# Selective scan: one product and one recurrence of 1024 columns per group in place of two interleaved halves of each

## The chip, the cores and the metric

One core of a Trainium2 chip runs the whole program. The metric is the device time in microseconds (us) of one execution, and a lower one is better.

## The reference

The program is two layers of a transformer-like net on four sequences of 1024 tokens, 128 features wide: attention and a mixture of experts, then a selective scan (a Mamba-like block) and a second mixture of experts. The change lies in the selective scan, of which this is the core:

```
def _selective_scan(u, A, B_sel, C_sel, delta):
    deltaA = jnp.exp(delta[..., None, None] * A[None, None])
    deltaB_u = delta[..., None, None] * B_sel[:, :, None, :] * u[..., None]

    def step(h, inp):
        a_t, bu_t, c_t = inp
        h = a_t * h + bu_t
        y_t = jnp.einsum('bdn,bn->bd', h, c_t)
        return (h, y_t)
```

For each of 128 features there are 16 states, and each state runs through the 1024 tokens of its sequence by h = a·h + bu. All arithmetic is fp32.

## The kernel before

The scan puts (feature, state) pairs on the 128 partitions and the 1024 tokens of a sequence along the free dimension. A **group** is 8 features × 16 states, so there are 16 groups for each sequence and 64 in all. For group n:

- SyncE loads `x_rep` (the input u, repeated over the states) from memory, one of 5 buffers.
- ScalarE (ACT) makes `da` = exp(delta·A), 1024 columns, three groups ahead, one of 5 buffers (line 2910).
- VectorE (DVE) makes the **product** `ps_bu` = `x_rep` · `ps_b` into PSUM (line 2658); `ps_b` lies in PSUM, `x_rep` in SBUF. It is made in two halves of 512 columns, c = 0 and c = 1.
- VectorE makes the **recurrence** `st` with `tensor_tensor_scan` from `da` (SBUF) and `ps_bu` (PSUM), also in two halves: `first_half` (line 2666) starts from 0, `second_half` (line 2672) from the last column of the first.
- GpSimd (POOL) makes `hc` = `st` · `crep`, 1024 columns, as soon as the whole recurrence of the group is there (line 2929). Both its inputs lie in SBUF.
- TensorE (PE) sums `hc` over the states into `ps_y`, for four groups at a time.

Each engine walks the same list, `scan_plan()`, and takes from it the steps that are its own. Between two groups VectorE has other work, of two kinds. The row statistics (`row_stats`, lines 156 and 160, one SBUF input each) stand in the list after a group's last instruction. The **small steps** are generators on a list `small`: `late_delta` (line 2763, 1024 columns, two SBUF inputs), `deviations` (five operations on 8 columns, lines 2771 to 2783), and the choice of an expert and of a token's place (`choose`, lines 1113 to 1137; `place`, lines 1157 to 1170). `between(3)` runs up to three of them at one point in each group. Most read two SBUF tensors.

The halves are interleaved. For group n VectorE issues: product c = 0 of n, the small steps, second half of n - 1, first half of n, product c = 1 of n. So no instruction needs the one right before it. POOL also issues indirect DMAs (lines 2936 and 1255), the product `brep` · `delta` (line 2947) and `y` · `z` (line 2954) between its `hc` products. At the turn to another sequence ScalarE copies `brep` into `ps_b` (line 2891), and VectorE's next product waits for that.

Of the kernel before, what the change touches and what calls it, by code (L numbers as in the profile page):

```python
# [11 lines left out]
ALU = mybir.AluOpType  # L12
# [4 lines left out]
BATCH, SEQ, HID = 4, 1024, 128  # L17
# [3 lines left out]
BANK = 512  # L21
# [1260 lines left out]
HALF = F0 // 2  # L1282
# [1018 lines left out]
NG = HID // FG  # L2301
NC2 = SEQ // BANK
# [4 lines left out]
NDA, AHEAD, NST_BUF = 5, 3, 4  # L2307

NX, NW = 5, 2
# [105 lines left out]
def selective_scan(nc, sems, a, u_mem, w_tap, w_in, x, h_t, h, spare, wo, marks, weights, loaded, mod_t, gate_bc, ident, eps,  # L2415
# [4 lines left out]
    with ExitStack() as ctx:  # L2420
# [6 lines left out]
        def mark(n, step=1):  # L2427
            return Mark(nc, sems, f"m_{n}", step, marks.pop())

        def sem(n):  # L2430
# [9 lines left out]
        raw, soft, delta = sb("raw"), sb("soft"), [begun_scan[3], sb("delta1")]  # L2440
        x_rep = [sb(f"x_rep{i}") for i in range(NX)]
        brep, crep = sb("brep"), [sb(f"crep{i}") for i in range(2)]
        da, st = [sb(f"da{i}") for i in range(NDA)], [sb(f"st{i}") for i in range(NST_BUF)]
        hc = [sb(f"hc{i}") for i in range(NHC)]
        y = wo[:, :, :, :].rearrange("p k j n -> p (k j n)")
# [11 lines left out]

        w_pe, y_pe = mark("w_pe"), mark("y_pe")

        act, delta_dve, bu_dve, half_dve, scan_dve, y_act = (  # L2460
            mark(n) for n in ("act", "delta", "bu", "half", "scan", "y"))

        y_pool, y_last, delta_b_pool = mark("y_pool"), mark("y_last"), mark("delta_b")

# [9 lines left out]
        for step in plan:  # L2474
            kind, key = step[0], step[1:]
            if step in turn and kind != "conv" or kind == "conv" and key[2] == 0:
                w_pe.add(step)
            if kind in ("u", "z", "raw", "turn") or kind == "rep" and (key[0] or key[1]):
                act.add(step)
            elif kind in ("turn3", "score", "back3", "join"):  # L2480
                act.add(step)
            elif kind == "norm3":
                norm3_act.add(key)
            elif kind == "norm":
                x_norm.add(key)
            elif kind == "soft":
                act.add(step), act.add(step), act.add(step)
            elif kind == "delta":
                delta_dve.add(step)
            elif kind == "delta_b":  # L2490
                (delta_dve if len(key) == 2 else delta_b_pool).add(step)
            elif kind == "b_in":
                act.add(step)
            elif kind == "group":
                for m in (da_act, half_dve, scan_dve, hc_pool):
                    m.add(key)
                for c in range(NC2):
                    bu_dve.add(key + (c,))
            elif kind == "sum":
                y_pe.add(key)  # L2500
            elif kind == "y":
                last_pe.add(key[0])
                for c in range(NC2):
                    for m in (y_act, y_pool) if key[0] < BATCH - 1 else (y_last,):
                        m.add(key + (c,))
            elif kind == "out":
                add_act.add(key)
# [29 lines left out]
        def behind(b, g, by):  # L2537

            n = b * NG + g - by
            return divmod(n, NG) if n >= 0 else None  # L2540
# [106 lines left out]
        def g_first(key):  # L2647
            return key[1] == 0

        def product(e, key, c):  # L2650
            n, cc = key[0] * NG + key[1], HALF[c]
            if c == 0:
                e.wait_ge(x_in[n % NX], (n // NX + 1) * 16)
            if n:

                m = (half_dve, scan_dve)[c]
                e.wait_ge(m.sem, m.at[behind(*key, 1)])
            e.tensor_tensor(ps_bu[:, cc], x_rep[n % NX][:, cc], ps_b[:, cc], ALU.mult).then_inc(bu_dve.sem, 1)  # L2658

        def first_half(e, key):  # L2660
            n, cc = key[0] * NG + key[1], HALF[0]
            e.wait_ge(bu_dve.sem, bu_dve.at[key + (0,)])
            e.wait_ge(da_act.sem, da_act.at[key])
            if behind(*key, NST_BUF):
                e.wait_ge(hc_pool.sem, hc_pool.at[behind(*key, NST_BUF)])
            e.tensor_tensor_scan(st[n % NST_BUF][:, cc], da[n % NDA][:, cc], ps_bu[:, cc], 0.0, ALU.mult, ALU.add).then_inc(half_dve.sem, 1)

        def second_half(e, key):
            n, cc = key[0] * NG + key[1], HALF[1]
            e.wait_ge(bu_dve.sem, bu_dve.at[key + (1,)])  # L2670
            e.wait_ge(half_dve.sem, half_dve.at[key])
            e.tensor_tensor_scan(st[n % NST_BUF][:, cc], da[n % NDA][:, cc], ps_bu[:, cc], st[n % NST_BUF][:, BANK - 1:BANK],  # L2672
                                 ALU.mult, ALU.add).then_inc(scan_dve.sem, 1)

        def vector(e):
            e.wait_ge(loaded, LATER * 16)
# [13 lines left out]
            for step in plan:  # L2690
# [14 lines left out]
                elif kind == "sums":  # L2705
                    b, n = key
# [12 lines left out]
                if kind == "delta" and len(key) == 1:  # L2719
                    small.append(late_delta(e, *key))  # L2720
                elif kind == "delta_b" and key[0] == 0:
                    at, cc = ("rep", 0) + key, part(key)
                    e.wait_ge(w_pe.sem, w_pe.at[at])
                    e.tensor_tensor(ps_b[:, cc], ps_w[turn[at] % NW][:, :], delta[0][:, cc], ALU.mult).then_inc(delta_dve.sem, 1)
                elif kind == "group":

                    if g_first(key):
                        if key[0]:
                            second_half(e, behind(*key, 1))
                        e.wait_ge(*b_ready(key[0]))  # L2730
                        product(e, key, 0)
                    else:
                        product(e, key, 0)
                        between(3)
                        second_half(e, behind(*key, 1))
                    first_half(e, key)
                    product(e, key, 1)
                    if key == (BATCH - 1, NG - 1):
                        second_half(e, key)
                elif kind == "y" and key[0] == BATCH - 1:  # L2740
                    b, = key
                    for c in range(NC2):
                        cc = slice(c * BANK, (c + 1) * BANK)
                        if c < NC2 - 1:
                            e.wait_ge(last_pe.sem, last_pe.at[b])
                        else:
                            e.wait_ge(y_pe.sem, y_pe.at[b, NG // SET - 1])
                        e.wait_ge(w_pe.sem, w_pe.at["out", b - 1, c])
                        e.wait_ge(act.sem, act.at["z", b, c])
                        e.tensor_tensor(y[:, cc], ps_y[c][:, :], z[b % 2][:, cc], ALU.mult).then_inc(y_last.sem, 1)  # L2750
                elif kind == "stats":
                    b, n = key
                    tile = b * TPB + n * 4
                    e.wait_ge(add_act.sem, add_act.at[key])
                    row_stats(e, x, stats, mv, range(tile, tile + 4), row_chain)
                    stats_at[key] = row_chain.n
# [583 lines left out]
```

## Time and profile before

| | us |
|---|---|
| median of 3 runs | 1818.52 (1814.84 to 1818.67) |
| the profiled execution, its own time | 1820.8 |
| its span, first to last instruction | 1819.1 |
| the scan, first product to the start of the last `hc` | 1330.1 to 1600.2 |
| VectorE busy over the span | 1152.2 |
| GpSimd busy over the span | 1346.1 |

The profiled execution is one run of its own, so its stretches are read as durations, and a sum of them is set against its own time. Instructions of VectorE that don't need each other overlap by a few hundredths of a us in the timeline: the next starts before the one before has ended. The distance from start to start is therefore what an instruction takes of the engine, called its pitch below.

### The profile page before, as it was taken

The page shows a single profiled execution, that of the slowest core. Times are in us where ns is not written, and L with a number is a line of the kernel's source. Part 1 is how long each engine was busy: PE and PEld are TensorE (multiplying, and loading weights), DVE is VectorE, ACT ScalarE, POOL GpSimd, SP SyncE. Part 2 cuts the span into 40 slices and gives each one's busy share as a digit, 9 for nine tenths or more (in the row PEclk, how much of TensorE's full clock was granted, in tenths as well). Part 3 has the DMA queues.
Part 4 walks back from the last instruction along what each step waited for, and adds up shares of the span by engine and source line. Part 5 has one row for each costly group of instructions (what it writes and reads, how often), then busy time and mean ns, then how long its engine had stood idle before and what let it go on. Part 6 is the DMA issues. An engine that isn't in the chain of part 4 may idle for free. (4 is left out here: it accounts for less than half of the span.)

```text
span 1819.1 us, 26796 instructions
## 1 busy us (share of the span) xinstructions
PE 1502.0 (83%) x8699; PEld 1034.9 (57%) x8699; DVE 1152.2 (63%) x2579; ACT 797.8 (44%) x1379; POOL 1346.1 (74%) x1154
## 2 busy tenths in 40 slices
PE   5899999999999999999999998988965664357970
PEld 3455556766556755656755657877833232136960
DVE  6866766566676575676566504755589998952224
ACT  2245444345444344444344453444486775323320
POOL 5587988788898698898788783536576657658376
PEclk7699999999999999999999998999977876667995
DMA  6333334231222122131131103024485555424333
GB/s 177 70 89 82 71 71 83 70 70 42 65 58 48 48 56 50 36 70 36 47 70 36 36 13 86 23 72 114 109 199 126 141 133 132 108 69 146 99 86 87
DMA packets 125761, 146.65 MB, mean 81 GB/s; under 512 B 15784, under 2 KB 84796, under 8 KB 125624
## 3 DMA queue, kind: packets, MB, share of 16 engines
q1 hardware_dynamic: 118456, 130.60, 29.3%
q0 software_dynamic: 7168, 14.34, 2.9%
q8 instruction: 72, 1.18, 0.3%
q14 instruction: 65, 0.53, 0.1%
HBM read 65.24 MB, written 29.42 MB: 52 GB/s over the span
## 5 line engine op out<-in xcount | busy, mean ns | idle before, releaser
L838 DVE CUSTOM_DVE_ANT_0 ring<-ring,mask 128x128 f32<-128x128 f32 (+7 forms) x512 | 383.8, 769 | 186.3 <-PE ring L700 185.9
L924 ACT ACTIVATE prob<-ring 128x512 f32<-128x512 f32 x576 | 315.2, 597 | 298.1 <-PE ring L715 294.5
L978 POOL TENSOR_TENSOR acc<-acc,prob 128x512 f32<-128x512 f32 x272 | 353.1, 1298 | 73.0 <-ACT prob L924 49.4
L731 PE MATMUL ps_o<-prob,v 128*64 128x256 f32 x2304 | 282.5, 387 | 3.9 <-issue 3.8
L700 PE MATMUL ring<-k,x 128*128 128x512 f32 (+3 forms) x768 | 252.0, 408 | 35.8 <-ACT prob L924 22.1
L714 PE MATMUL ring<-x,k 128*128 128x512 f32 x576 | 258.1, 448 | 24.6 <-DVE neg_m L838 15.4
L715 PE MATMUL ring<-x,k 128*128 128x512 f32 x576 | 229.4, 398 | 0.0
L700 PEld LDWEIGHTS ring<-k,x 128*128 128x128 f32 x768 | 137.3, 198 | 144.5 <-ACT prob L924 50.9
L731 PEld LDWEIGHTS ps_o<-prob,v 128*64 128x64 f32 x2304 | 154.6, 137 | 106.5 <-issue 39.6
L2929 POOL TENSOR_TENSOR m_hc<-m_st,m_crep 128x1024 f32<-128x1024 f32 x64 | 150.8, 2357 | 71.7 <-DVE m_st L2672 64.0
L975 POOL TENSOR_TENSOR acc<-prob 128x512 f32<-128x512 f32 x144 | 184.4, 1281 | 8.5 <-ACT prob L924 7.2
L945 POOL TENSOR_TENSOR other<-other,sin 128x512 f32<-128x512 f32 x96 | 136.3, 1420 | 59.2 <-DVE other L817 58.6
L714 PEld LDWEIGHTS ring<-x,k 128*128 128x128 f32 x576 | 109.2, 190 | 99.4 <-issue 44.3
L947 POOL TENSOR_TENSOR rot<-rot,other 128x512 f32<-128x512 f32 x96 | 129.2, 1346 | 7.5
L715 PEld LDWEIGHTS ring<-x,k 128*128 128x128 f32 x576 | 109.8, 191 | 19.7 <-issue 7.3
L830 DVE TENSOR_TENSOR rot<-rot,other 128x512 fp32r<-128x512 f32 x64 | 73.2, 1143 | 69.5 <-ACT other L906 69.5
L963 POOL TENSOR_SCALAR_AFFINE_SELECT prob<-prob 128x512 f32<-128x512 f32 x128 | 91.3, 713 | 25.6 <-ACT prob L924 24.5
L816 DVE TENSOR_TENSOR rot<-ring,cos 128x512 f32<-128x512 f32 x96 | 66.3, 690 | 60.1 <-PE ring L682 59.7
L3155 POOL DMA_INDIRECT c_got<-slots_out,f_slot x64 | 65.9, 1030 | 46.3 <-issue 40.6
L743 PE MATMUL ps_l<-acc,v_one 128*64 128x256 f32 x576 | 87.5, 381 | 2.8 <-POOL acc L978 2.7
L1255 POOL DMA_INDIRECT slots_in<-attn_t,f_slot x64 | 63.0, 985 | 31.8 <-issue 15.5
L2658 DVE TENSOR_TENSOR m_ps_bu<-m_x_rep,m_ps_b 128x512 f32<-128x512 f32 x128 | 82.5, 680 | 4.7 <-ACT m_ps_b L2891 4.4
(414 smaller groups left out, 2816.1 us busy)
## 6 DMA issues: line engine op xcount, KB each, us to landing
x<-other SPq DMA_DIRECT2D x256, 128.0 KB, 2.3
m_x_rep<-u_mem SPq DMA_DIRECT2D x64, 512.0 KB, 4.7
x<-rot SPq DMA_DIRECT2D x128, 128.0 KB, 2.3
sorted_in<-zeros SPq DMA_DIRECT2D x3, 1548.0 KB, 11.9
e_sorted<-sorted_in SPq DMA_DIRECT2D x18, 258.0 KB, 3.7
sorted_out<-e_hid SPq DMA_DIRECT2D x18, 256.0 KB, 2.2
slots_in<-zeros SPq DMA_DIRECT2D x2, 2048.0 KB, 8.7
slots_out<-wo SPq DMA_DIRECT2D x16, 256.0 KB, 2.4
```

The lines of the kernel that those rows point to most:

```text
L700: mm = e.matmul(ps[:, c0:c1], x1[g % 2][:, h, qs], k1[g % 3][:, c0:c1], start=True, stop=True)
L714: e.matmul(banks(step, BANK), k1[g % 3][:, ks], x1[g % 2][:, :, qs], start=True, stop=False)
L715: e.matmul(banks(step, BANK), k2[g % 3][:, ks], x2[g % 2][:, :, qs], start=False, stop=True).then_inc(s2_pe.sem, 1)
L731: mm = e.matmul(ps_o[s * D:(s + 1) * D, qb % 2 * 2 * P:(qb % 2 + 1) * 2 * P], v[g % 2][:, kb, :], prob[i % NPROB][:, s * 2 * P:(s + 1) * 2 ...
L838: e.tensor_tensor_reduce(ps, ps, mask_1[:, SEQ - n:SEQ], 1.0, -3.0 * NEG, ALU.add, ALU.min, neg_m[g % 2][:, c, h, qb % QPC:qb % QPC + 1]). ...
L924: e.activation(prob[i % NPROB][:, :], banks(("s2",) + key, BANK), ACT.Exp, scale=-1.0).then_inc(s2_exp.sem, 1)
L945: e.tensor_tensor(other[i][:, :], other[i][:, :], sin[:, cc], ALU.mult).then_inc(rotated.sem, 1)
L947: e.tensor_tensor(rot[i][:, :], rot[i][:, :], other[i][:, :], ALU.add).then_inc(rotated.sem, 1)
L963: e.affine_select(tile[:, :], tile[:, :], [[0, G], [1, P]], ALU.is_ge, 0.0, base=0, channel_multiplier=-1).then_inc(causal.sem, 1)
L975: e.tensor_tensor(total[:, :], first[:, :], tile[:, :], ALU.add).then_inc(summed.sem, 1)
L978: e.tensor_tensor(total[:, :], total[:, :], tile[:, :], ALU.add).then_inc(summed.sem, 1)
L2929: e.tensor_tensor(hc[(b * NG + g) % NHC][:, :], st[r][:, :], crep[b % 2][:, :], ALU.mult).then_inc(hc_pool.sem, 1)
```

## The change

`product` makes all 1024 columns in one instruction, and `states` runs the whole recurrence in one `tensor_tensor_scan` from 0. The product of group n waits for the recurrence of n - 1, which reads `ps_bu`, and the recurrence of n waits for its product. The small steps stay between product and recurrence. The semaphore of the first half is gone. ScalarE, TensorE, GpSimd and SyncE have the same instructions in the same order.

```diff
-        def product(e, key, c):
-            n, cc = key[0] * NG + key[1], HALF[c]
-            if c == 0:
-                e.wait_ge(x_in[n % NX], (n // NX + 1) * 16)
+        def product(e, key):
+            n = key[0] * NG + key[1]
+            e.wait_ge(x_in[n % NX], (n // NX + 1) * 16)
             if n:
-
-                m = (half_dve, scan_dve)[c]
-                e.wait_ge(m.sem, m.at[behind(*key, 1)])
-            e.tensor_tensor(ps_bu[:, cc], x_rep[n % NX][:, cc], ps_b[:, cc], ALU.mult).then_inc(bu_dve.sem, 1)
+                e.wait_ge(scan_dve.sem, scan_dve.at[behind(*key, 1)])
+            e.tensor_tensor(ps_bu[:, :], x_rep[n % NX][:, :], ps_b[:, :], ALU.mult).then_inc(bu_dve.sem, NC2)
 
-        def first_half(e, key):
-            n, cc = key[0] * NG + key[1], HALF[0]
-            e.wait_ge(bu_dve.sem, bu_dve.at[key + (0,)])
+        def states(e, key):
+            n = key[0] * NG + key[1]
+            e.wait_ge(bu_dve.sem, bu_dve.at[key + (NC2 - 1,)])
             e.wait_ge(da_act.sem, da_act.at[key])
             if behind(*key, NST_BUF):
                 e.wait_ge(hc_pool.sem, hc_pool.at[behind(*key, NST_BUF)])
-            e.tensor_tensor_scan(st[n % NST_BUF][:, cc], da[n % NDA][:, cc], ps_bu[:, cc], 0.0, ALU.mult, ALU.add).then_inc(half_dve.sem, 1)
-
-        def second_half(e, key):
...
+            e.tensor_tensor_scan(st[n % NST_BUF][:, :], da[n % NDA][:, :], ps_bu[:, :], 0.0, ALU.mult, ALU.add).then_inc(scan_dve.sem, 1)
...
                     if g_first(key):
-                        if key[0]:
-                            second_half(e, behind(*key, 1))
                         e.wait_ge(*b_ready(key[0]))
-                        product(e, key, 0)
-                    else:
-                        product(e, key, 0)
+                    product(e, key)
+                    if not g_first(key):
                         between(3)
-                        second_half(e, behind(*key, 1))
-                    first_half(e, key)
-                    product(e, key, 1)
-                    if key == (BATCH - 1, NG - 1):
-                        second_half(e, key)
+                    states(e, key)
```

In the listings below a line number is that of the kernel it belongs to; `tensor_tensor_scan` is listed as SCALAR_TENSOR_TENSOR. VectorE in the first sequence, groups with no small steps, before (2658 is a product, 2672 a second half, 2666 a first half):

```order
L2658 TENSOR_TENSOR m_ps_bu<-m_x_rep,m_ps_b 128x512 x2
L2672 SCALAR_TENSOR_TENSOR m_st<-m_da,m_st,m_ps_bu 128x512
L2666 SCALAR_TENSOR_TENSOR m_st<-m_da,m_ps_bu 128x512
L2658 TENSOR_TENSOR m_ps_bu<-m_x_rep,m_ps_b 128x512 x2
L2672 SCALAR_TENSOR_TENSOR m_st<-m_da,m_st,m_ps_bu 128x512
L2666 SCALAR_TENSOR_TENSOR m_st<-m_da,m_ps_bu 128x512
```

The same engine and place in the changed kernel (2654 is the product, 2662 the recurrence):

```order
L2654 TENSOR_TENSOR m_ps_bu<-m_x_rep,m_ps_b 128x1024
L2662 SCALAR_TENSOR_TENSOR m_st<-m_da,m_ps_bu 128x1024
L2654 TENSOR_TENSOR m_ps_bu<-m_x_rep,m_ps_b 128x1024
L2662 SCALAR_TENSOR_TENSOR m_st<-m_da,m_ps_bu 128x1024
L2654 TENSOR_TENSOR m_ps_bu<-m_x_rep,m_ps_b 128x1024
```

Six instructions for two groups became four, each of which needs the result of the one in front of it.

VectorE at the first `deviations` (its five small steps, 2771 to 2783), before. The two products in front of a small step are c = 1 of group n - 1 and c = 0 of group n, and the second half of n - 1 (2672) comes behind the steps:

```order
L2666 SCALAR_TENSOR_TENSOR m_st<-m_da,m_ps_bu 128x512
L2658 TENSOR_TENSOR m_ps_bu<-m_x_rep,m_ps_b 128x512 x2
L2771 SCALAR_TENSOR_TENSOR m_nmr<-mv,m_rstd 128x8
L2774 TENSOR_TENSOR m_nmr<-m_nmr,m_rstd 128x8
L2777 TENSOR_SCALAR m_nmr<-m_nmr 128x8
L2672 SCALAR_TENSOR_TENSOR m_st<-m_da,m_st,m_ps_bu 128x512
L2666 SCALAR_TENSOR_TENSOR m_st<-m_da,m_ps_bu 128x512
L2658 TENSOR_TENSOR m_ps_bu<-m_x_rep,m_ps_b 128x512 x2
L2780 TENSOR_TENSOR m_rstd<-m_rstd,m_nmr 128x8
L2783 SCALAR_TENSOR_TENSOR m_nmr<-mv,m_rstd 128x8
```

The same place in the changed kernel, where the five steps are lines 2753 to 2765:

```order
L2654 TENSOR_TENSOR m_ps_bu<-m_x_rep,m_ps_b 128x1024
L2753 SCALAR_TENSOR_TENSOR m_nmr<-mv,m_rstd 128x8
L2756 TENSOR_TENSOR m_nmr<-m_nmr,m_rstd 128x8
L2759 TENSOR_SCALAR m_nmr<-m_nmr 128x8
L2662 SCALAR_TENSOR_TENSOR m_st<-m_da,m_ps_bu 128x1024
L2654 TENSOR_TENSOR m_ps_bu<-m_x_rep,m_ps_b 128x1024
L2762 TENSOR_TENSOR m_rstd<-m_rstd,m_nmr 128x8
L2765 SCALAR_TENSOR_TENSOR m_nmr<-mv,m_rstd 128x8
L2662 SCALAR_TENSOR_TENSOR m_st<-m_da,m_ps_bu 128x1024
```

The second half of the group before has moved from behind the small steps to a place ahead of the product, so the whole recurrence of n - 1 is complete when that product starts, and the small steps come one instruction of 1024 columns after it.

## Rows read from the trace of the kernel before

**Rows 1.** the page: busy time, share of the span and instructions of each engine

```profile
PE 1502.0 (83%) x8699; PEld 1034.9 (57%) x8699; DVE 1152.2 (63%) x2579; ACT 797.8 (44%) x1379; POOL 1346.1 (74%) x1154
```

**Rows 2.** busy time of each engine in stretches of the scan

```profile
1330.00:1360.00 30.00, 20.58 (x95) 11.35 (x94) 29.80 (x53) 22.77 (x30) 26.04 (x17) 0.88 0.88 207
...
1530.00:1603.00 73.00, 29.63 (x163) 16.10 (x165) 70.66 (x109) 27.80 (x40) 57.59 (x33) 0.66 0.39 103
```

**Rows 3.** waits of VectorE (DVE), 1330 to 1600: us in total, times, longest

```profile
DVE m_ps_bu L2658 <- ACT m_ps_b L2891: 4.4, 2, 2.7
DVE m_delta L2763 <- ACT m_soft L2886: 3.7, 2, 3.2
DVE f_prod L1157 <- PE m_ps_w L1146: 2.3, 1, 2.3
DVE stats L156 <- ACT first_h L2872: 1.7, 1, 1.7
```

**Rows 4.** timeline, VectorE: start us, us, engine, line, operation

```profile
1336.05 1.26 DVE L2658 TENSOR_TENSOR m_ps_bu<-m_x_rep,m_ps_b 128x512 f32<-128x512 f32 x2
1337.22 1.27 DVE L2672 TENSOR_TENSOR_SCAN m_st<-m_da,m_st,m_ps_bu 128x512 f32<-128x512 f32 x1
1338.41 1.19 DVE L2666 TENSOR_TENSOR_SCAN m_st<-m_da,m_ps_bu 128x512 f32<-128x512 f32 x1
1339.53 1.26 DVE L2658 TENSOR_TENSOR m_ps_bu<-m_x_rep,m_ps_b 128x512 f32<-128x512 f32 x2
```

**Rows 5.** single lines, duration in ns as min/median/max

```profile
L2658 DVE TENSOR_TENSOR m_ps_bu<-m_x_rep,m_ps_b x128: 667/678/697, 1330.1 to 1596.3; 128x512 f32<-128x512 f32 x128
L2666 DVE TENSOR_TENSOR_SCAN m_st<-m_da,m_ps_bu x64: 1186/1196/1220, 1330.8 to 1595.2; 128x512 f32<-128x512 f32 x64
L2929 POOL TENSOR_TENSOR m_hc<-m_st,m_crep x64: 2334/2356/2385, 1336.2 to 1600.2; 128x1024 f32<-128x1024 f32 x64
L1130 DVE TENSOR_TENSOR_SCAN f_upto<-f_keep,f_mask x2: 292/292/292, 1480.8 to 1554.6; 128x64 f32<-128x64 f32 x2
L2763 DVE SCALAR_TENSOR_TENSOR m_delta<-m_raw,m_soft x2: 1226/1226/1227, 1368.1 to 1508.7; 128x1024 f32<-128x1024 f32 x2
```

**Rows 6.** timeline, VectorE, a product and what follows without needing it

```profile
1349.96 0.68 DVE L2658 TENSOR_TENSOR m_ps_bu<-m_x_rep,m_ps_b 128x512 f32<-128x512 f32 x1
1350.54 0.86 DVE L156 BATCH_NORM_STATS2 stats<-first_h 128x6 f32<-128x128 f32 x4
```

**Rows 7.** timeline, VectorE, a scan right behind its own product

```profile
1398.87 0.70 DVE L2658 TENSOR_TENSOR m_ps_bu<-m_x_rep,m_ps_b 128x512 f32<-128x512 f32 x1 [2.72 <-ACT m_ps_b L2891]
1399.60 1.22 DVE L2666 TENSOR_TENSOR_SCAN m_st<-m_da,m_ps_bu 128x512 f32<-128x512 f32 x1
```

**Rows 8.** timeline, all engines, small steps beside POOL's product

```profile
1369.20 1.27 DVE L2672 TENSOR_TENSOR_SCAN m_st<-m_da,m_st,m_ps_bu 128x512 f32<-128x512 f32 x1
...
1370.56 2.36 POOL L2929 TENSOR_TENSOR m_hc<-m_st,m_crep 128x1024 f32<-128x1024 f32 x1 [1.49 <-DVE m_st L2672]
...
1371.50 1.27 DVE L2658 TENSOR_TENSOR m_ps_bu<-m_x_rep,m_ps_b 128x512 f32<-128x512 f32 x2
...
1372.68 0.26 DVE L2771 SCALAR_TENSOR_TENSOR m_nmr<-mv,m_rstd 128x8 f32<-128x8 f32 x1
...
1372.97 0.17 DVE L2774 TENSOR_TENSOR m_nmr<-m_nmr,m_rstd 128x8 f32<-128x8 f32 x1
```

**Rows 9.** timeline, all engines, a small step late behind POOL

```profile
1411.51 2.35 POOL L2929 TENSOR_TENSOR m_hc<-m_st,m_crep 128x1024 f32<-128x1024 f32 x1
...
1412.35 1.53 DVE L2771 SCALAR_TENSOR_TENSOR m_nmr<-mv,m_rstd 128x8 f32<-128x8 f32 x1
```

**Rows 10.** timeline, VectorE, the last such pair of small steps

```profile
1579.73 0.27 DVE L2780 TENSOR_TENSOR m_rstd<-m_rstd,m_nmr 128x8 f32<-128x8 f32 x1
```

**Rows 11.** timeline, all engines, the last recurrence and product

```profile
1597.05 1.28 DVE L2672 TENSOR_TENSOR_SCAN m_st<-m_da,m_st,m_ps_bu 128x512 f32<-128x512 f32 x1
...
1600.17 2.36 POOL L2929 TENSOR_TENSOR m_hc<-m_st,m_crep 128x1024 f32<-128x1024 f32 x1
```

More of the change, by code:

```diff
@@ L2458, in selective_scan @@
         w_pe, y_pe = mark("w_pe"), mark("y_pe")
-        act, delta_dve, bu_dve, half_dve, scan_dve, y_act = (
-            mark(n) for n in ("act", "delta", "bu", "half", "scan", "y"))
+        act, delta_dve, bu_dve, scan_dve, y_act = (mark(n) for n in ("act", "delta", "bu", "scan", "y"))
         y_pool, y_last, delta_b_pool = mark("y_pool"), mark("y_last"), mark("delta_b")
@@ L2494, in selective_scan @@
             elif kind == "group":
-                for m in (da_act, half_dve, scan_dve, hc_pool):
+                for m in (da_act, scan_dve, hc_pool):
                     m.add(key)
@@ L2665, in first_half @@
                 e.wait_ge(hc_pool.sem, hc_pool.at[behind(*key, NST_BUF)])
-            e.tensor_tensor_scan(st[n % NST_BUF][:, cc], da[n % NDA][:, cc], ps_bu[:, cc], 0.0, ALU.mult, ALU.add).then_inc(half_dve.sem, 1)
-        def second_half(e, key):
[L2669 to L2673, printed above, removed]
+            e.tensor_tensor_scan(st[n % NST_BUF][:, :], da[n % NDA][:, :], ps_bu[:, :], 0.0, ALU.mult, ALU.add).then_inc(scan_dve.sem, 1)
         def vector(e):
```

## The prediction

> **What bounds the kernel now.** I read the page's busy times first [rows 1]. Over the whole span TensorE is busiest, at 83%, but this change touches one stage of 270 us, so the average says little. The busy times by stretch [rows 2] are the second view. In the scan VectorE is busy for 29.80 of 30 us at its start and 70.66 of 73 us at its end, while POOL has 26.04 and 57.59. The third view is the list of VectorE's waits in the stage [rows 3]: 12.1 us in all, none of them for POOL. VectorE therefore sets the pace of the scan. Nothing else comes after it until its last recurrence is there, since POOL, the sum, the output and the routing of the last sequence all hang on it. I count a us more on VectorE as a us more in the end, less what the waits and POOL's own lateness swallow.
>
> **The plain group.** A group repeats every 3.48 us (1336.05 to 1339.53) [rows 4]: two products of 0.585 us each, a second half of 1.19 and a first half of 1.12, from start to start. These pitches are shorter than the durations (0.678 for a product, 1.196 for a first half) [rows 5]. A product whose successor doesn't need it has 0.58 us to the next start [rows 6]. The one place where a recurrence comes right behind the product that it needs has 0.73 us [rows 7], and the recurrence there takes 1.22.
>
> The 512 further columns of a product cost about 0.55: a VectorE operation of 1024 columns takes 1.226 against 0.678 [rows 5]. For a recurrence, 64 columns take 0.292 and 512 take 1.196, so 512 more cost 0.904 / 448 × 512 = 1.03 [rows 5]. The new product needs 0.73 + 0.55 = 1.28. The new recurrence needs its 1.22, 1.03 more, and the same gap of 0.03 before the next product: 2.28. The group is then 3.56 us, 0.08 more than now. Two instructions fewer are saved, but the overlap of each with its successor is gone, and that overlap is worth slightly more. About 32 of the 64 groups are plain: +2.6 us. In the 22 groups with small steps the product is followed by a step that doesn't need it, so they take 0.58 + 0.55 + 2.28 = 3.41 plus the steps, against 3.48: -0.07 each, -1.5 in all. The 10 with row statistics have an independent neighbour behind the recurrence: -0.05 each, -0.5. Sum of the instructions themselves: **+0.6**. The bounds are wide here. If a wait for the instruction in front costs nothing, the group is 1.13 + 2.15 = 3.28 (row pitch 0.58 + 0.55, 1.12 + 1.03), and if a full-length recurrence costs 2.08 ns a column more instead of 2.02 (1.07 for 512), it is 3.60.
>
> The Trainium skill speaks against this term: VectorE: DVE Perf Modes, "Rules for kernel authors", says to minimize the count of operations and not the semaphores, because the flush behind each comes anyway. By that rule the sum below would lose its first term and gain the rival "count alone". The rows here disagree in part, since a product has 0.58 or 0.73 us to its successor depending on whether it is waited for.
>
> **The small steps.** This is the term that decides. A step with two SBUF inputs doesn't finish while POOL's `hc` product runs. At 1372.68 the first step of `deviations` takes 0.26 us where its like takes 0.17, and it ends at 1372.94, just after `hc` (1370.56 + 2.36 = 1372.92) [rows 8]. At 1412.35 the same step takes 1.53 us and ends at 1413.88. POOL had begun late there, at 1411.51, and ended at 1413.86 [rows 9]. So it waits out POOL's product. Now the wait is mostly 0.09 us, because 2.2 us of work lie between the end of a second half (1370.47) and the small steps (1372.68), and `hc` starts 0.09 us after that end and lasts 2.36.
>
> In the changed kernel the recurrence of n - 1 ends, `hc` of n - 1 starts 0.09 later and ends 2.45 after it. VectorE starts product n 0.03 after it and reaches the small steps 1.13 later, that is 1.16 after it. The first step with two SBUF inputs must wait until 2.45. It ends at 2.47 where it would have ended at 1.33, so it loses 1.13 us against 0.09 now: **1.04 us for each such stop**. What I counted in the timeline, 22 stops from 1368.1 to 1579.9 (the pair at 1579.73 is the last) [rows 10]:
>
> - 11 stops whose first step has two SBUF inputs and where POOL is on time: 11 × 1.04 = 11.4.
> - 2 where a one-input reduction of some 0.24 us comes first: 0.85 each, 1.7.
> - 3 right after POOL's `y` product, where `hc` is already late, as in [rows 9]. They lose 1.1 to 1.8 us now and would lose 0.8 to 1.1: -1.2.
> - the `late_delta` at 1368.1, which has its wait for ScalarE ahead of it and would meet POOL's product: +0.9.
> - the other 5, where the first steps read one SBUF tensor or POOL is done: +1.0 together.
>
> Sum **+13.8**. The bounds: none of it if VectorE is let through, and 2.3 us for each of the three stops at `y` if POOL goes from one product into the next ahead of the waiting step (+7).
>
> **What is swallowed.** Of the 12.1 us of waits [rows 3], 3.2 hangs on a small step in the group before, one group of work away, and moves with it. The 2.3 for a TensorE count and the 1.7 for `first_h` wait for ScalarE and TensorE, which run by themselves there; VectorE comes to them later by its own delay and with up to a second half more work behind it. I take 2.5 of these 4.0. The 4.4 for `ps_b` stay within 0.3, since there the wait starts from a step that comes nearer. Together **-2.2**, between 0 and -12.1.
>
> At the end POOL is late by itself. The last second half ends at 1598.33 and the last `hc` starts at 1600.17, 1.84 us later instead of 0.09 [rows 11], as POOL has an indirect DMA in each of the last groups. POOL's pace there doesn't change, so part of VectorE's delay is covered: **-1.0** of at most 1.75.
>
> TensorE, ScalarE and SyncE get the same work. The buffer `x_rep` comes free at the end of one product instead of its second half, which isn't later relative to the next load.
>
> **Sum.** 0.6 + 13.8 - 2.2 - 1.0 = +11.2 us. The profiled execution took 1820.8 us and would be 1832.0. The median of the runs shown lies 2.3 below it, so the forecast is 1818.5 + 11.2 = 1830.
>
> **The rivals.**
>
> - *POOL blocks the small steps* (the forecast): 1830. Chance 0.66.
> - *Count alone.* A wait for the instruction in front costs nothing, and two instructions fewer save their pitch. The plain group is 3.28 in place of 3.56, 32 × 0.28 = 9.0 less, and the other 32 groups lose the one dependent gap that is left in each, 32 × 0.13 = 4.1 less. 11.2 - 13.1 = -1.9: 1817. Against it stands 0.73 against 0.58 us. It decides if the plain group comes out under 3.3. Chance 0.08.
> - *VectorE is let through* (faster). The steps are tiny and finish beside POOL's product. The 13.8 fall away, 11.2 - 13.8 = -2.6: 1816. Every long step that I looked at ended within 0.1 us of POOL's product, which speaks against it. The stops would have to cost under 2.6 us together for the kernel to be faster at all. Chance 0.08.
> - *The other engines set the stage.* All 12.1 us of waits swallow VectorE's delay in place of 2.2: 0.6 + 13.8 - 12.1 - 1.0 = +1.3, 1820. The wait of 3.2 that moves with the steps speaks against it. Chance 0.10.
> - *POOL goes ahead in a row.* At `y` and `brep` the step waits for two products of POOL, +7: 1837. Chance 0.08.
>
> **How the numbers follow.** Runs of this kernel differ by about 0.2% (3.6 us), and that is what a measurement can tell from no change. The range of 1820 to 1837 takes in the forecast with a price of 0.5 to 1.6 us for a stop, the fourth and the fifth case, and leaves out the second and third and a little of the rest. Of the second and third I give half to faster by over 0.2% (the plain sum is near the edge): 0.08 with a little for the unknown. Within 0.2% are the other half and most of the fourth: 0.15. Slower has 0.77.
>
> **What would show it.** In the changed kernel's timeline the product takes about 1.23 us and the recurrence 2.25, a plain group repeats every 3.56 us (3.28 is the second case). The first two-input small step of a stop takes about 1.3 us and ends with POOL's `hc` (0.17 is the third case). The waits of [rows 3] keep their 3.2, and those for TensorE and `first_h` shrink below 2 together. The stage from the first product to the last `hc` grows from 270 to about 281 us, and nothing outside it changes. The prediction is wrong if the stage grows and a later one gives it back, or if POOL's `hc` starts much later than 0.09 us after the recurrence.

## The result and the profile after

The changed kernel takes 1831.84 us (median of 4 runs, 1831.24 to 1833.15), the kernel before 1818.38 (4 runs). The ratio is 1.0076, with a 95% interval of 1.0062 to 1.0089: slower by 13.5 us. The forecast was 1830, and +11.2 us as a difference. The profiled execution has a span of 1831.4 us against 1819.1, so the terms below explain 12.3 us; the other 1.2 lie between single executions and medians.

The page's busy times, as in [rows 1]:

```profile
PE 1497.7 (82%) x8699; PEld 1033.4 (56%) x8699; DVE 1167.2 (64%) x2451; ACT 797.8 (44%) x1379; POOL 1347.5 (74%) x1154
```

VectorE has 15 us more busy time and 128 instructions fewer, and POOL's is 1.4 us more. Busy time by stretch, which answers to [rows 2] (stretch and its length, then PE, PEld, DVE, ACT, POOL):

```profile
1330.00:1360.00 30.00, 22.18 (x97) 12.16 (x96) 28.89 (x37) 22.86 (x30) 27.01 (x18) 0.85 0.85 201
...
1530.00:1615.00 85.00, 34.46 (x178) 18.79 (x178) 81.83 (x76) 30.71 (x46) 63.29 (x35) 0.64 0.41 102
```

VectorE is busy for 28.89 of 30 us and 81.83 of 85: it still sets the pace. The two merged lines, with durations in ns as min/median/max:

```profile
L2654 DVE TENSOR_TENSOR m_ps_bu<-m_x_rep,m_ps_b x64: 1204/1229/1230, 1331.0 to 1609.2; 128x1024 f32<-128x1024 f32 x64
...
L2662 DVE TENSOR_TENSOR_SCAN m_st<-m_da,m_ps_bu x64: 2259/2286/2289, 1332.2 to 1610.5; 128x1024 f32<-128x1024 f32 x64
```

The product takes 1.229 us, as forecast (1.23), and the recurrence 2.286, which is 0.04 over the forecast 2.25. The timeline of plain groups, which answers to [rows 4], shows what was not forecast:

```profile
1339.91 2.29 DVE L2662 TENSOR_TENSOR_SCAN m_st<-m_da,m_ps_bu 128x1024 f32<-128x1024 f32 x1
1342.33 1.23 DVE L2654 TENSOR_TENSOR m_ps_bu<-m_x_rep,m_ps_b 128x1024 f32<-128x1024 f32 x1
1343.60 2.29 DVE L2662 TENSOR_TENSOR_SCAN m_st<-m_da,m_ps_bu 128x1024 f32<-128x1024 f32 x1
1346.02 1.23 DVE L2654 TENSOR_TENSOR m_ps_bu<-m_x_rep,m_ps_b 128x1024 f32<-128x1024 f32 x1
```

A plain group repeats every 3.69 us (1342.33 to 1346.02), where 3.48 was measured before and 3.56 forecast. The recurrence follows its product by 1.27 us, as forecast, but the product starts 0.13 us after the recurrence's recorded end (1339.91 + 2.29 = 1342.20), not 0.03.

The stop at the first `deviations`, which answers to [rows 8]. POOL's `hc` is line 2911 here, `brep` is line 2929:

```profile
1375.67 2.34 POOL L2911 TENSOR_TENSOR m_hc<-m_st,m_crep 128x1024 f32<-128x1024 f32 x1 [1.36 <-DVE m_st L2662]
1375.71 1.23 DVE L2654 TENSOR_TENSOR m_ps_bu<-m_x_rep,m_ps_b 128x1024 f32<-128x1024 f32 x1
1376.85 1.18 DVE L2753 SCALAR_TENSOR_TENSOR m_nmr<-mv,m_rstd 128x8 f32<-128x8 f32 x1
...
1377.97 2.33 POOL L2929 TENSOR_TENSOR m_brep<-m_brep,m_delta 128x1024 f32<-128x1024 f32 x1
1378.07 2.26 DVE L2756 TENSOR_TENSOR m_nmr<-m_nmr,m_rstd 128x8 f32<-128x8 f32 x1
```

POOL starts `hc` 0.04 us before VectorE starts the product. The first small step starts 1.14 us into the product and ends at 1378.03, just after POOL's 1378.01. It took 1.18 us, 0.26 before. POOL's `brep` starts at 1377.97, the next small step at 1378.07, and that step is held for another 2.26 until `brep` is done. VectorE's waits, as in [rows 3]:

```profile
DVE m_delta L2745 <- ACT m_soft L2868: 3.8, 1, 3.8
DVE m_ps_bu L2654 <- DVE m_st L2662: 0.5, 1, 0.5
```

Of 12.1 us of waits for other engines 3.8 are left, plus 0.5 for itself. The last recurrence and product, as in [rows 11]:

```profile
1610.51 2.29 DVE L2662 TENSOR_TENSOR_SCAN m_st<-m_da,m_ps_bu 128x1024 f32<-128x1024 f32 x1
...
1612.88 2.34 POOL L2911 TENSOR_TENSOR m_hc<-m_st,m_crep 128x1024 f32<-128x1024 f32 x1 [0.18 <-DVE m_st L2662]
```

The recurrence ends at 1612.80 and `hc` starts at 1612.88: the 1.84 us by which POOL was late are gone.

To compare term by term I added up VectorE's time from the first product's start to the last recurrence's end in the timeline: for each instruction the distance to the next start, less the wait noted there, by kind.

| us, first product to last recurrence | before | after | change | forecast |
|---|---|---|---|---|
| products | 76.5 | 78.0 | +1.5 | |
| recurrences | 147.6 | 152.0 | +4.3 | |
| row statistics | 11.9 | 11.8 | -0.2 | |
| these three | 236.1 | 241.7 | +5.7 | +0.6 |
| small steps | 20.1 | 35.8 | +15.7 | +13.8 |
| waits | 12.1 | 4.3 | -7.8 | -2.2 |
| POOL late at the end | 1.8 | 0.1 | -1.8 | -1.0 |
| sum | 270.1 | 281.9 | +11.8 | +11.2 |

The stage up to the start of the last `hc` grew from 270.1 us (1330.09 to 1600.17) to 281.9 (1330.96 to 1612.88). Outside it the spans differ by 0.5 us.

### The profile page after: what moved, and what is told of

Same layout as the page of the kernel before. It is cut to its first block and busy times, and to the rows that moved or that the text cites. A ratio compares the mean times of both kernels' runs of the same rounds, so it can differ in the third digit from the quotient of the medians.

```text
span 1831.4 us, 26608 instructions
## 1 busy us (share of the span) xinstructions
PE 1497.7 (82%) x8699; PEld 1033.4 (56%) x8699; DVE 1167.2 (64%) x2451; ACT 797.8 (44%) x1379; POOL 1347.5 (74%) x1154
## 3 DMA queue, kind: packets, MB, share of 16 engines
q8 instruction: 72, 1.18, 0.3%
## 5 line engine op out<-in xcount | busy, mean ns | idle before, releaser
L714 PE MATMUL ring<-x,k 128*128 128x512 f32 x576 | 258.5, 449 | 24.7 <-DVE neg_m L838 15.4
L2662 DVE TENSOR_TENSOR_SCAN m_st<-m_da,m_ps_bu 128x1024 f32<-128x1024 f32 x64 | 146.2, 2284 | 1.5
## 6 DMA issues: line engine op xcount, KB each, us to landing
sorted_in<-zeros SPq DMA_DIRECT2D x3, 1548.0 KB, 12.1
```

The lines of the kernel that those rows point to most:

```text
L714: e.matmul(banks(step, BANK), k1[g % 3][:, ks], x1[g % 2][:, :, qs], start=True, stop=False)
L2662: e.tensor_tensor_scan(st[n % NST_BUF][:, :], da[n % NDA][:, :], ps_bu[:, :], 0.0, ALU.mult, ALU.add).then_inc(scan_dve.sem, 1)
```

## Experiments

The theory is that VectorE's small steps wait for POOL's products, and that the change moved them to where such a product has just begun. The rival is that the merged instructions cost the time themselves, by depending on each other.

**Halves, with the small steps behind the second half.** Nothing is merged; only the steps move.

```diff
                         product(e, key, 0)
-                        between(3)
                         second_half(e, behind(*key, 1))
+                        between(3)
```

> The kernel before (halves, interleaved) with one edit: the small steps stand behind the second half of the group before instead of ahead of it. Nothing is merged. If POOL's product blocks the small steps, the first step of a stop slips in before POOL starts and the second one, which starts about 0.1 us after the recurrence is complete, waits some 2.3 us. About 17 of the 22 stops have such a second step: 39 us, less the 7 us of such waits that are there already, so +20 to +35 us (1840 to 1853) and VectorE's time in small steps grows from 20 to about 50 us. If the merged kernel is slow only because its instructions are merged and depend on each other, this kernel is the same as before within 4 us.

Measured: 1844.22 us against 1819.49, ratio 1.0135 (1.0117 to 1.0152), +24.7 us, inside the expected 20 to 35. The small steps grew from 20.1 to 55.1 us and the waits shrank from 12.1 to 4.3, while products (76.1) and recurrences (147.8) stayed. The timeline at the first `deviations`:

```profile
1372.77 1.27 DVE L2672 TENSOR_TENSOR_SCAN m_st<-m_da,m_st,m_ps_bu 128x512 f32<-128x512 f32 x1
...
1373.96 0.14 DVE L2771 SCALAR_TENSOR_TENSOR m_nmr<-mv,m_rstd 128x8 f32<-128x8 f32 x1
1374.13 2.34 POOL L2929 TENSOR_TENSOR m_hc<-m_st,m_crep 128x1024 f32<-128x1024 f32 x1
1374.13 2.36 DVE L2774 TENSOR_TENSOR m_nmr<-m_nmr,m_rstd 128x8 f32<-128x8 f32 x1
...
1376.43 2.34 POOL L2947 TENSOR_TENSOR m_brep<-m_brep,m_delta 128x1024 f32<-128x1024 f32 x1
1376.52 2.27 DVE L2777 TENSOR_SCALAR m_nmr<-m_nmr 128x8 f32<-128x8 f32 x1
```

The first step starts before the second half's recorded end and is through in 0.14 us. POOL starts `hc` at 1374.13, and the second step, which starts at the same time, is held for the 2.34 us of it. The third is held for `brep`. So moving the steps alone, with all instructions as before, makes the kernel slower by more than the merge did. The rival's "same as before" is out.

**POOL's product cut to 64 columns, in both kernels.** From the seventh group on POOL multiplies only the first 64 columns of `st`; the other columns of `hc` are left as they were, so this part of the computation is left out in both.

```diff
-                    e.tensor_tensor(hc[(b * NG + g) % NHC][:, :], st[r][:, :], crep[b % 2][:, :], ALU.mult).then_inc(hc_pool.sem, 1)
+                    some = slice(0, SEQ if behind(b, g, NHC) is None else 64)
+                    e.tensor_tensor(hc[(b * NG + g) % NHC][:, some], st[r][:, some], crep[b % 2][:, some], ALU.mult).then_inc(hc_pool.sem, 1)
```

In the changed kernel:

> The changed kernel with POOL's product st times crep cut to 64 of its 1024 columns from the seventh group on (the rest of hc is left as it was, so that part of the computation is left out). Port theory: the stops have nothing to wait for but POOL's brep and y products, VectorE's small steps fall from 35.8 us to 13 to 16 us, the plain group stays at 3.68 us, and the time falls by 15 to 23 us to 1809 to 1817. If the small steps are slow for another reason (their place behind a long instruction), they stay above 30 us and the time above 1826.

In the kernel before:

> The kernel before with the same cut of POOL's product to 64 columns (that part of the computation is left out). With e2 it shows what the merge costs when POOL is out of the way. Port theory: small steps fall from 20.1 to 13 to 16 us, the time by 2 to 7 us to 1811 to 1816, and the merged kernel with the same cut is 0 to 6 us slower than this one, since merged products and recurrences take 5.8 us more and the waits of VectorE swallow part of it. If the merge itself is what costs, the gap between the two cut kernels stays at 13 us.

Measured: merged 1811.60 us, ratio 0.9951 (0.9934 to 0.9968); halves 1805.02, ratio 0.9917 (0.9899 to 0.9935). The gap of 13.5 us between the two kernels is 6.6 us with POOL out of the way. The six runs of the merged one lie between 1805.5 and 1815.1, so this gap is known to a few us only; between the two profiled executions the stage differs by 5.8. The small steps take 16.9 us in the merged kernel (35.8 with the full product) and 13.1 in halves (20.1). The port theory had 13 to 16 for both, so the merged kernel's lies 0.9 above; the gap of 6.6 us is 0.6 above its 0 to 6, and clear of the rival's 13. The merged kernel's first `deviations`, with the short `hc` (2912) and `brep` (2930):

```profile
1373.57 0.32 POOL L2912 TENSOR_TENSOR m_hc<-m_st,m_crep 128x64 f32<-128x64 f32 x1 [2.95 <-DVE m_st L2662]
1373.62 1.23 DVE L2654 TENSOR_TENSOR m_ps_bu<-m_x_rep,m_ps_b 128x1024 f32<-128x1024 f32 x1
1373.85 2.35 POOL L2930 TENSOR_TENSOR m_brep<-m_brep,m_delta 128x1024 f32<-128x1024 f32 x1
1374.76 1.47 DVE L2753 SCALAR_TENSOR_TENSOR m_nmr<-mv,m_rstd 128x8 f32<-128x8 f32 x1
```

`hc` takes 0.32 us and is gone before the small steps come, but now `brep` lies there (1373.85 to 1376.20), and the step at 1374.76 ends at 1376.23 with it. In halves the same steps run free, and one of the next pair meets `brep` for its last 0.5 us:

```profile
1367.49 0.32 POOL L2930 TENSOR_TENSOR m_hc<-m_st,m_crep 128x64 f32<-128x64 f32 x1 [3.09 <-DVE m_st L2672]
...
1369.61 0.16 DVE L2771 SCALAR_TENSOR_TENSOR m_nmr<-mv,m_rstd 128x8 f32<-128x8 f32 x1
...
1371.73 2.35 POOL L2948 TENSOR_TENSOR m_brep<-m_brep,m_delta 128x1024 f32<-128x1024 f32 x1
...
1373.57 0.53 DVE L2780 TENSOR_TENSOR m_rstd<-m_rstd,m_nmr 128x8 f32<-128x8 f32 x1
```

The product and recurrence terms are those of the uncut kernels (78.4 and 152.0 merged, 76.5 and 147.6 in halves), so the cost of the merge itself is about 6 us whatever POOL does. The halved kernel gained more than I expected, 14.5 us and not 2 to 7. Of its span's 15.3 us the stage on VectorE gives 7.8, POOL's lateness at the end 1.8, and the last `hc` itself 2.0; 2.6 lie before the first product, where nothing was edited, and 1.2 after. The waits stayed (3.9 us for `ps_b`, 3.2 for `m_soft`, 11.3 of 12.1 in all).

**The wait for `x_rep` taken out from in front of the product.** It is issued ahead of the recurrence instead. In the same edit the recurrence's wait for its product moved behind the one for `da`.

```diff
-            e.wait_ge(x_in[n % NX], (n // NX + 1) * 16)
+            if n == 0:
+                e.wait_ge(x_in[0], 16)
...
-            e.wait_ge(bu_dve.sem, bu_dve.at[key + (NC2 - 1,)])
+            if n + 1 < BATCH * NG:
+                e.wait_ge(x_in[(n + 1) % NX], ((n + 1) // NX + 1) * 16)
             e.wait_ge(da_act.sem, da_act.at[key])
+            e.wait_ge(bu_dve.sem, bu_dve.at[key + (NC2 - 1,)])
```

> The changed kernel with the wait for x_rep of the next group issued ahead of the recurrence, so that only one wait stands in front of the product. It is about the 0.13 us between the end of a recurrence and the next product, where 0.03 was forecast. If the second wait costs it, the gap falls to about 0.04, the plain group from 3.68 to 3.59 and the time by 3 to 6 us. If the recurrence's completion comes late by itself, group and time stay within 0.02 us and 3 us.

Measured: 1836.62 us against 1819.49, ratio 1.0106 (1.0081 to 1.0130), about 5.5 us slower than the changed kernel. Neither case came out:

```profile
1341.82 2.29 DVE L2665 TENSOR_TENSOR_SCAN m_st<-m_da,m_ps_bu 128x1024 f32<-128x1024 f32 x1 [0.20 <-DVE m_ps_bu L2655]
1344.21 1.23 DVE L2655 TENSOR_TENSOR m_ps_bu<-m_x_rep,m_ps_b 128x1024 f32<-128x1024 f32 x1
1345.64 2.29 DVE L2665 TENSOR_TENSOR_SCAN m_st<-m_da,m_ps_bu 128x1024 f32<-128x1024 f32 x1 [0.20 <-DVE m_ps_bu L2655]
```

In the changed kernel the recurrence waits in the order `hc`, `da`, product: the late one comes last. In this kernel the order is product, `hc`, `da`, `x_rep`, and the three that come after the late one cost 0.16 us together, 0.05 each on average. The program also has one separate wait instruction more there (the product's wait stands in one of its own, `hc` and `da` in a second), and this run can't part that from the number of waits. The edit tested two things at once, and the second one was an accident. The next run takes it apart.

**The product's two waits swapped.**

```diff
-            e.wait_ge(x_in[n % NX], (n // NX + 1) * 16)
             if n:
                 e.wait_ge(scan_dve.sem, scan_dve.at[behind(*key, 1)])
+            e.wait_ge(x_in[n % NX], (n // NX + 1) * 16)
```

> The changed kernel with the two waits of the product swapped, so that the one for the recurrence is tested last and the one for x_rep has been passed before. In the kernel with the x_rep wait taken away the pitch from recurrence to product fell from 2.42 to 2.39, and a wait that stood in front of others raised the pitch from product to recurrence from 1.26 to 1.43. If each wait tested after the late one costs 0.03 to 0.06 us, the pitch is 2.39 here and the time 2 us less, 1829 to 1831. If the order doesn't matter, it stays 2.42.

Measured: 1828.84 us against 1817.24, ratio 1.0065 (1.0048 to 1.0082). The group:

```profile
1340.11 2.29 DVE L2662 TENSOR_TENSOR_SCAN m_st<-m_da,m_ps_bu 128x1024 f32<-128x1024 f32 x1
1342.48 1.23 DVE L2654 TENSOR_TENSOR m_ps_bu<-m_x_rep,m_ps_b 128x1024 f32<-128x1024 f32 x1
1343.75 2.29 DVE L2662 TENSOR_TENSOR_SCAN m_st<-m_da,m_ps_bu 128x1024 f32<-128x1024 f32 x1
```

The pitch from recurrence to product has a median of 2.38 us (2.42 before the swap; in 51 of the 64 groups a product comes right behind, so 2 us). The ratio moved from 1.0076 to 1.0065, the right way and size, but within the intervals. What is left of the gap is 0.08 to 0.09 us, the same that POOL needs from the end of a recurrence to its `hc`.

**A tiny instruction between recurrence and product.**

```diff
                     states(e, key)
+                    e.memset(tiny[:, :], 0.0)
```

> The changed kernel with a memset of one column on VectorE between each recurrence and the next product, which needs nothing. If the 0.13 us between them is the engine's restart after a wait, the tiny instruction overlaps the end of the recurrence and the product follows within 0.05 us of that end. If the recurrence's result counts as complete only 0.1 us after its recorded end, the product starts as late as before, 2.40 to 2.42 us after the recurrence's start, and the plain group stays at 3.66 to 3.68 us.

Measured: 1832.05 us against 1817.24. It is one run, so only its timeline is used.

```profile
1342.63 2.29 DVE L2663 TENSOR_TENSOR_SCAN m_st<-m_da,m_ps_bu 128x1024 f32<-128x1024 f32 x1
1344.86 0.06 DVE L2723 MEMSET m_tiny<- 128x1 f32 x1
1345.05 1.23 DVE L2655 TENSOR_TENSOR m_ps_bu<-m_x_rep,m_ps_b 128x1024 f32<-128x1024 f32 x1
```

The memset starts at 1344.86, before the recurrence's recorded end at 1344.92, yet the product starts at 1345.05, 2.42 us after the recurrence's start and 0.13 us after its end, as without the memset. So not every instruction that follows a recurrence comes late, only the one that waits for its result. How much of the gap is a late result and how much is taking up again after a wait, this run doesn't tell. The gap belongs to the dependence and can be covered only by work that is long enough and doesn't need it, as in the interleaved halves.

**Products halved, recurrence whole.**

```diff
-            e.tensor_tensor(ps_bu[:, :], x_rep[n % NX][:, :], ps_b[:, :], ALU.mult).then_inc(bu_dve.sem, NC2)
+            for cc in HALF:
+                e.tensor_tensor(ps_bu[:, cc], x_rep[n % NX][:, cc], ps_b[:, cc], ALU.mult).then_inc(bu_dve.sem, 1)
```

> The changed kernel with the product in two halves of 512 columns again, both behind the whole recurrence of the group before. It parts the merged product from the merged recurrence. By the rows after the change a product of two halves takes 0.585 + 0.71 = 1.30 us against 1.26, so +1 to +3 us (1832 to 1835), with the recurrence's pitch of 2.42 and the small steps' 36 us unchanged. If the merged product were the cause of the slowdown, this kernel would gain 4 us or more.

Measured: 1831.57 us against 1817.24, ratio 1.0075 (1.0058 to 1.0091). That is the changed kernel's ratio of 1.0076 and not 1 to 3 us more; nor is it the gain of 4 us. In the profiled executions the stage is 1.7 us longer.

```profile
1341.38 2.29 DVE L2663 TENSOR_TENSOR_SCAN m_st<-m_da,m_ps_bu 128x1024 f32<-128x1024 f32 x1
1343.77 1.29 DVE L2655 TENSOR_TENSOR m_ps_bu<-m_x_rep,m_ps_b 128x512 f32<-128x512 f32 x2
1345.09 2.29 DVE L2663 TENSOR_TENSOR_SCAN m_st<-m_da,m_ps_bu 128x1024 f32<-128x1024 f32 x1
```

Two halves take 1.32 us (1343.77 to 1345.09) against 1.27 for the whole, and the recurrence's pitch is 2.39. Merging the product is worth 0.05 to 0.07 us a group; merging the recurrence, and with it the end of the interleaving, is what costs. For the pitch of 2.39 in place of 2.42 the compiled program offers a reason: the wait for `x_rep` is carried by the first half product itself here, and no longer shares a wait instruction with the late one. With the wait for `x_rep` taken out from in front of the product the pitch was 2.39 too.

**One small step per group, behind the recurrence.**

```diff
+                    states(e, key)
                     if not g_first(key):
-                        between(3)
-                    states(e, key)
+                        between(1)
```

> The changed kernel with one small step per group instead of up to three, placed behind the recurrence instead of between product and recurrence. Port theory: a single step starts before POOL's product and gets through, so VectorE's small steps fall from 35.8 to 15 to 22 us (the rest is flushed in bulk at a few places and still waits). The time falls by 6 to 16 us, less what VectorE's waits for later results grow by (the steps come later): 1816 to 1828. If it is the number of steps or their place in the order that costs, and not POOL's product, the small steps stay above 30 us and the time at 1830 or more.

Measured: 1830.02 us against 1817.24, ratio 1.0068 (1.0051 to 1.0085). That is outside what I expected on the time (1816 to 1828), and the small steps take 31.3 us and not 15 to 22. Both numbers fall on the side that I had given to the rival (above 30 us, 1830 or more), so they don't speak for POOL; only the timeline does. A single step gets through where POOL is on time:

```profile
1380.81 2.29 DVE L2662 TENSOR_TENSOR_SCAN m_st<-m_da,m_ps_bu 128x1024 f32<-128x1024 f32 x1
...
1383.01 0.14 DVE L2759 TENSOR_SCALAR m_nmr<-m_nmr 128x8 f32<-128x8 f32 x1
1383.17 2.36 POOL L2911 TENSOR_TENSOR m_hc<-m_st,m_crep 128x1024 f32<-128x1024 f32 x1 [1.33 <-DVE m_st L2662]
...
1383.22 1.23 DVE L2654 TENSOR_TENSOR m_ps_bu<-m_x_rep,m_ps_b 128x1024 f32<-128x1024 f32 x1
```

The step starts at 1383.01, before the recurrence's end at 1383.10, and takes 0.14 us; `hc` starts at 1383.17. But where POOL is late the step meets a product that is under way, and where the list empties the rest at one place (a flush), the second step is held again:

```profile
1441.35 2.33 POOL L2929 TENSOR_TENSOR m_brep<-m_brep,attn_t 128x1024 f32<-128x1024 f32 x1
1442.56 1.15 DVE L2753 SCALAR_TENSOR_TENSOR m_nmr<-mv,m_rstd 128x8 f32<-128x8 f32 x1
1443.65 2.33 POOL L2911 TENSOR_TENSOR m_hc<-m_st,m_crep 128x1024 f32<-128x1024 f32 x1
1443.74 2.27 DVE L2756 TENSOR_TENSOR m_nmr<-m_nmr,m_rstd 128x8 f32<-128x8 f32 x1
```

`brep` holds the first step, which takes 1.15 us, and `hc`, which starts at 1443.65 right behind it, the second for 2.27. In this scan ten small steps of 8 and 64 columns take over 1.1 us each, where their free time is under 0.3, and each ends within 0.13 us of the end of a POOL product. Twice the order is the other way: `late_delta` starts at 1437.98 and takes its free time of 1.20, and `hc`, which starts 0.17 later, takes 3.24 in place of 2.34. VectorE's waits rose from 4.3 to 9.5. So the stops are still POOL's, and the cure is poor.

**Halves, with four long stops moved away from POOL's `brep` and `y`.**

```diff
-        joined.setdefault(at + 7, []).append(("dev1", b))
+        joined.setdefault(at + (9 if b == 2 else 8), []).append(("dev1", b))
...
-             16: [("score", b, 1)], 19: [("choose", b)]}
+             16: [("score", b, 1)], 20: [("choose", b)]}
...
-    for at in range(NG, 20):
+    for at in range(NG, 21):
```

> The kernel before with four long stops moved away from POOL's brep and y products: the deviations of the third and fourth sequence start two groups and one group later in the list, the choice of an expert one group later. Nothing else changes. Port theory: the stops at 1377.0, 1412.4, 1475.2 and 1548.4, which now cost 2.1, 1.4, 1.1 and 1.7 us above their free time, fall to about 0.1 each. VectorE's small steps fall from 20.1 to 14 to 16 us; since two of the stops stand ahead of waits for other engines, 2 to 5 us of the time go (1813 to 1817). If POOL's product isn't what they wait for, the small steps stay at 20 us and the time the same.

Measured: 1816.56 us (12 runs) against 1818.46 (17 runs), ratio 0.9993 (0.9983 to 1.0002): no difference that this tells. The small steps fell only from 20.1 to 18.5 us. The stop at 1475.2 became free, the one at 1412.4 fell from 1.53 to 0.39 us and the one of 1.97 us to 1.00. The deviations of the third sequence, moved away from `brep`, ran into this, and two later steps of the choice (line 1133) are held for some 0.7 us each:

```profile
1376.36 1.05 POOL L2936 DMA_INDIRECT attn_t<-sorted_out,sorted_slot  x1 [0.16 <-issue]
...
1377.04 2.77 DVE L2771 SCALAR_TENSOR_TENSOR m_nmr<-mv,m_rstd 128x8 f32<-128x8 f32 x1
1377.44 2.35 POOL L2929 TENSOR_TENSOR m_hc<-m_st,m_crep 128x1024 f32<-128x1024 f32 x1
```

The step starts during an indirect DMA of POOL (1376.36 to 1377.41) and is held until `hc`, which starts behind it, ends at 1379.79. What VectorE gained it then waited: 5.6 us for `ps_b` (4.4 before) and 2.7 for `first_h` (1.7). All its waits are 13.2 us, 1.1 more than before. The engines that VectorE waits for at these places had not become faster.

## Why the prediction was right

The direction, the place and the main term were right, and the time lay 1.8 us from the forecast. Two other terms were off by over 5 us each, in opposite directions.

- **What bounds the kernel.** VectorE sets the pace of the scan: held up. The stage grew by 11.8 us and nothing later gave it back.
- **The plain group, +0.6.** The step that failed is "the same gap of 0.03 before the next product": a mis-sized term, with the mechanism right. The three kinds cost 5.7 us. In 51 groups a product follows the recurrence, after 2.42 us in place of the 2.28 of the sum: 0.10 more gap and 0.04 more duration, 6.9 us together, of which shorter product pitches and a slightly slower group before (224.1 us for products and recurrences, not 64 × 3.48) take back some. Of the gap of 0.13 us, 0.03 to 0.04 is one more wait tested after the late one (the swapped waits); the other 0.09 is what an instruction that waits for a recurrence needs, on POOL as on VectorE. I had taken the gap from the only dependent pair in the old trace, product to recurrence, though the 0.09 us from second half to POOL's `hc` stood in [rows 8]. With 0.09 the group would have been 3.62.
- **The rule on the count of operations** (the Trainium skill, VectorE: DVE Perf Modes, "Rules for kernel authors"). Merging a product gains 0.05 to 0.07 us a group where both halves stand together, so the count does count a little. The waits aren't free here: 0.58 us to a successor that doesn't wait, 0.73 to one that does [rows 6, 7], and 0.03 to 0.05 for a further wait tested after the late one.
- **The small steps, +13.8.** Measured +15.7. Single stops cost nearly what was worked out: 1.18 us for a step of 0.17, ending with POOL's `hc`, where 1.31 was forecast; the product starts 0.10 later behind the recurrence, and the step meets that much less of `hc`. What the sum left out is `brep`, where a second step was held for 2.26 us three times in place of once, 4.2 us more. The POOL-goes-ahead rival had named that place, but not what happens there: the step that waits during `hc` ends with `hc` (1378.03), and it is the next step, which starts 0.10 us after `brep`, that waits for `brep`. At `y` there was no second stop, and those stops got shorter, as forecast.
- **What is swallowed, -2.2.** A mis-sized term too: -7.8. The step that failed is "the 4.4 for `ps_b` stay within 0.3". They went to nothing, as did the 2.3 and the 1.7. At the first turn ScalarE's copy into `ps_b` starts at 1398.46, 0.6 us later than before (1397.83), while VectorE gets to its next product at 1400.73 and not, as before, at 1396.15 with 2.72 us to wait. At the other two ScalarE is there first and waits for VectorE's product (1.78 and 1.77 us). Its copy of 1.03 us then runs beside the recurrence of 2.29, where before only a second half of 1.27 stood between the last product and the next sequence's first:

```profile
1542.15 2.29 DVE L2662 TENSOR_TENSOR_SCAN m_st<-m_da,m_ps_bu 128x1024 f32<-128x1024 f32 x1
1542.21 1.03 ACT L2873 ACTIVATE m_ps_b<-m_brep 128x1024 f32<-128x1024 f32 x1 [1.77 <-DVE m_ps_bu L2654]
```

The 3.2 that was to move with the small steps did, and is 3.8. The run with the four stops moved shows the same from the other side.
- **POOL at the end, -1.0.** Measured -1.8, the whole of what was there.

The two errors nearly cancel (+5.1 and -5.6), and so in part do the other two (+1.9 and -0.8). That the sum is 0.6 us off is luck; its terms were not that good. Not settled is why what waits for a recurrence starts 0.09 us after its recorded end and what waits for a product after 0.03. The place of the result doesn't explain it: the small step at 1372.68 writes SBUF too, and the step that needs it starts 0.03 after its end [rows 8]. Two differences are left. One is the operation. The other is how VectorE's wait is put in the compiled program, where the product's wait for the recurrence stands in a separate wait instruction and the recurrence carries its wait for the product itself. No run here parts these, but POOL's `hc`, which carries its wait for the recurrence itself, starts 0.08 to 0.09 after it as well.

## What to carry to other kernels

Before merging interleaved halves, look at what stands between them and where it then falls against the other engine that reads SBUF: the larger part of the price here was not the merged instructions (5.7 us) but tiny steps that came to stand right behind the start of a 2.4 us GpSimd product (15.7). Where two instructions need each other, the wait between them shows only once nothing else fills it. Put the late wait first in the source, so that it is tested last.

## What the runs showed of the hardware

- A VectorE step with two SBUF inputs that comes while GpSimd multiplies 1024 columns from SBUF hardly gets on until that product is done. A step of 8 columns ends 0.02 to 0.04 us after it, one of 64 columns 0.08 to 0.14. The `late_delta` of 1024 columns that starts at 1371.13 in the changed kernel, during an `hc` that ends at 1372.30, ends at 1373.38. A one-input `tensor_scalar` of 8 columns waited too (line 2759: 1.18 us at 1449.2 in the changed kernel). When VectorE is first, GpSimd's product waits (3.24 us in place of 2.34, in the run with one small step per group). This agrees with the Trainium skill, SBUF — State Buffer, "Who interferes with whom".
- Between two GpSimd products that follow each other without a gap, the step that is waiting gets through: at 1378.03, 1450.37 and 1525.21 in the changed kernel, and fifteen times more in the other runs, it ends 0.02 to 0.03 us after the first product and doesn't wait for the second. In the changed kernel the step behind it then meets `brep` (2.26 us each time). I had expected one stop there, and the rival had the waiting step lose to the next product.
- A small step that starts during an indirect DMA of GpSimd can be held over the product behind it as well: 2.77 us at 1377.04 in the last run, 2.98 at 1599.69 in the kernel before, 3.11 at 1522.24 with one small step per group. The instruction held at 1599.69 is free in the changed kernel (0.27 us at 1615.91), where it starts during an indirect DMA too. What decides is not shown.
- Instructions of VectorE that don't need each other overlap by 0.09 us. One that needs a product starts 0.03 to 0.04 us after the product's end, one that needs a recurrence 0.08 to 0.13 after its end.
- A wait that is tested after the one that comes last cost 0.16 us for three in front of a recurrence and 0.03 to 0.04 for one in front of a product. Carried by the product itself, with the late wait in a wait instruction ahead of it, it cost nothing that shows (2.39 us with and without it).
